# Split keys and queries kept in DRAM in the order of the stationary rows, each part twice, and loaded with one transfer over 128 partitions

## What is computed

```python
def _L0_xattn_ref(query, key, value, adj, mask, ...):
    Q, K, V = heads(query, Wq, bq), heads(key, Wk, bk), heads(value, Wv, bv)   # (B, 16, 512, 16)
    scores = einsum('bhqd,bhkd->bhqk', Q, K) / sqrt(16)
    scores = where(mask == 0, -inf, scores + adj)
    out = einsum('bhqk,bhkd->bhqd', softmax(scores), V)
    ...
x = x + _L0_attn_ref(_layernorm(x), ...)                  # Mamba-2
x = x + _L0_xattn_ref(_layernorm(x), ctx_1024, ctx_1024, adj, mask, ...)
x = x + _L0_ffn_ref(_layernorm(x), ...)
```

## Time and profile before

| | us |
|---|---|
| median of 3 runs | 1343.73 (1340.27 to 1345.88) |
| span of the profiled execution | 1348.2 |
| TensorE busy in it | 1190.5 (88%) |
| VectorE, ScalarE, GpSimd busy | 1001.0, 778.5, 635.0 |

### The profile page before, as it was taken

How to read it: one execution, slowest core, us unless ns; L and a number is a source line. 1 busy time by engine, 2 the same in 40 slices (tenths; PEclk the granted TensorE clock), 3 DMA queues, 4 the chain that set the end, 5 groups by cost and what they waited for, 6 DMA issues and landing times. The chain is left out here.

```text
span 1348.2 us, 29867 instructions
## 1 busy us (share of the span) xinstructions
PE 1190.5 (88%) x10284; PEld 833.2 (62%) x10284; DVE 1001.0 (74%) x2529; ACT 778.5 (58%) x1444; POOL 635.0 (47%) x554
## 2 busy tenths in 40 slices
PE   5688999899979999899989998999989998977387
PEld 2355567676757676666757665767767676755244
DVE  5767787788867887778767886888867886655386
ACT  2125577567655676557746766667545765566232
POOL 4561474346631683346532773168234663120365
PEclk9788899999988999889988999999988998899699
DMA  6043114300531033201430053104220142011511
GB/s 194 1 110 85 35 44 106 107 21 25 142 102 33 24 95 102 75 8 60 113 102 25 25 142 103 33 25 108 74 81 21 29 107 79 25 48 33 196 55 73
DMA packets 101524, 96.52 MB, mean 72 GB/s; under 512 B 17184, under 2 KB 76832, under 8 KB 100096
## 3 DMA queue, kind: packets, MB, share of 16 engines
q1 hardware_dynamic: 92912, 76.42, 19.0%
q0 software_dynamic: 6240, 17.57, 5.5%
q10 hardware_dynamic: 2224, 0.62, 0.2%
HBM read 71.49 MB, written 27.26 MB: 73 GB/s over the span
## 5 line engine op out<-in xcount | busy, mean ns | idle before, releaser
L891 ACT ACTIVATE T<-T,nmx 128x512 f32<-128x512 f32 x512 | 368.8, 724 | 249.2 <-DVE nmx L1257 245.8
L1257 DVE CUSTOM_DVE_ANT_0 T<-ps,am 128x512 f32<-128x512 f32 x512 | 346.6, 685 | 151.5 <-PE ps L680 149.6
L688 PE MATMUL pt<-ident,T 128*128 128x128 f32 x2048 | 336.4, 290 | 14.0 <-ACT PT L882 13.2
L688 PEld LDWEIGHTS pt<-ident,T 128*128 128x128 f32 x2048 | 240.2, 147 | 123.2 <-issue 93.4
L882 ACT COPY PT<-pt 128x512 f32<-128x512 f32 x352 | 201.8, 573 | 15.9 <-PE pt L688 15.2
L680 PE MATMUL ps<-k_st,q_st 64*128 64x512 f32 x512 | 135.8, 523 | 60.4 <-DMA q_st<-q_d 29.8
L1373 POOL TENSOR_TENSOR dmask<-triu,dA 128x1024 fp32r<-128x1024 f32 x64 | 132.1, 2129 | 49.7 <-DVE dA L1101 49.6
L705 PE MATMUL po<-PT,va 128*32 128x128 f32 x4096 | 140.1, 278 | 10.2 <-issue 6.2
L680 PEld LDWEIGHTS ps<-k_st,q_st 64*128 64x128 f32 x512 | 50.3, 192 | 136.4 <-issue 43.9
L1411 POOL TENSOR_TENSOR rr<-se,nhalf 128x1 f32<-128x1 f32 x32 | 22.2, 693 | 234.1 <-DVE se L1187 220.1
L705 PEld LDWEIGHTS po<-PT,va 128*32 128x32 f32 x4096 | 106.1, 110 | 33.2 <-issue 32.1
(11 more groups left out here) (212 smaller groups left out, 2030.1 us busy)
## 6 DMA issues: line engine op xcount, KB each, us to landing
k_st<-k_d SPq DMA_DIRECT2D x256, 64.0 KB, 2.2
q_st<-q_d SPq DMA_DIRECT2D x256, 64.0 KB, 2.4
am<-in_mask SPq DMA_DIRECT2D x8, 1024.0 KB, 5.4
k_d<-kp SPq DMA_DIRECT2D x32, 256.0 KB, 2.6
am<-in_adj POOLq DMA_DIRECT2D x8, 1024.0 KB, 10.6
q_d<-qp SPq DMA_DIRECT2D x128, 64.0 KB, 1.6
x_in<-in_x SPq DMA_DIRECT2D x8, 512.0 KB, 4.4
ctx_in<-in_ctxT SPq DMA_DIRECT2D x8, 512.0 KB, 4.5
```

Of the source, the lines that this page charges most:

```text
L688: ins = pe.transpose(pt[u % 2][:, kt * P:(kt + 1) * P], T[:, u % RING, kt * P:(kt + 1) * P], ident[:, :])
L891: act.activation(T[:, u % RING, :], T[:, u % RING, :], ACT.Exp, bias=nmx[:, u % RING:u % RING + 1], scale=-1.0).then_inc(sems["probs"], 1)
L1257: dve.tensor_tensor_reduce(T[:, u % RING, :], ps[(a * UNITS + u) % S_BANKS][:, :], ams[a % 2][:, qt, :], -1.0, 3e38, ALU.add, ALU.min, nmx ...
```

## The change

The DRAM tensors get the shape of the rows: `q_d[b, tile, pair, head of pair, copy, number, query]` and `k_d[b, pair, head of pair, copy, number, key]`. Each part is stored twice, to the two copies that hold it, with the loop over channel halves outside and over the four copies inside. A load is then one transfer over 128 partitions. A k store goes from 4 transfers of 256 KB to 8, a q store from 4 of 64 KB to 8; a key group is loaded with 1 transfer in place of 8, a query tile with 1 of 512 KB in place of 8 of 64 KB. The bytes loaded stay, the bytes stored double. Semaphore counts follow.

```diff
-        q_d = nc.dram_tensor("q_d", (B, C, 2, E, P), F32, kind="Internal").ap()
-        k_d = nc.dram_tensor("k_d", (B, 2, E, S), F32, kind="Internal").ap()
+        q_d = nc.dram_tensor("q_d", (B, C, HP, 2, 4, AD, P), F32, kind="Internal").ap()
+        k_d = nc.dram_tensor("k_d", (B, HP, 2, 4, AD, S), F32, kind="Internal").ap()
...
                 def k_in(b, g):
-                    for r, hl in enumerate((0, 1, 0, 1)):
-                        src = k_d[b, hl, g * HG * AD:(g + 1) * HG * AD, :].rearrange("(n h d) s -> h d n s", h=2, d=AD)
-                        for h in range(2):
-                            sp.dma_start(k_st[(4 * h + r) * AD:(4 * h + r + 1) * AD, HG // 2 * g:HG // 2 * (g + 1), :].bitcast(F32),
-                                         src[h]).then_inc(sems[f"k_in{g}"], 16)
+                    n = slice(HG // 2 * g, HG // 2 * (g + 1))
+                    sp.dma_start(k_st[:, n, :].bitcast(F32), k_d[b, n].rearrange("n h r d s -> (h r d) n s")).then_inc(sems[f"k_in{g}"], 16)
 
                 def q_in(b, c):
-                    for r, hl in enumerate((0, 0, 1, 1)):
-                        src = q_d[b, c, hl].rearrange("(n h d) s -> h d n s", h=2, d=AD)
-                        for h in range(2):
-                            sp.dma_start(q_st[(4 * h + r) * AD:(4 * h + r + 1) * AD, c % 2, :, :].bitcast(F32), src[h]).then_inc(sems[f"q_in{c % 2}"], 16)
+                    sp.dma_start(q_st[:, c % 2, :, :].bitcast(F32), q_d[b, c].rearrange("n h r d s -> (h r d) n s")).then_inc(sems[f"q_in{c % 2}"], 16)
...
                     if k == "rload":
-                        sp.wait_ge(sems["k_out"], at("k_out", b, 16 * 4))
+                        sp.wait_ge(sems["k_out"], at("k_out", b, 16 * 8))
...
-                        for hl in range(2):
-                            for kt in range(KE):
-                                sp.dma_start(k_d[b, hl, kt * P:(kt + 1) * P, :], kp[:, hl, kt, :].bitcast(F32)).then_inc(sems["k_out"], 16)
+                        for kt in range(KE):
+                            for r, hl in enumerate((0, 1, 0, 1)):
+                                sp.dma_start(k_d[b, HP // KE * kt:HP // KE * (kt + 1), :, r].rearrange("n h d s -> (n h) d s"), kp[:, hl, kt, :].bitcast(F32)).then_inc(sems["k_out"], 16)
...
-                        for hl in range(2):
-                            for kt in range(KE):
-                                sp.dma_start(q_d[b, c, hl, kt * P:(kt + 1) * P, :], qp[:, hl, kt, :].bitcast(F32)).then_inc(sems["q_out"], 16)
+                        for kt in range(KE):
+                            for r, hl in enumerate((0, 0, 1, 1)):
+                                sp.dma_start(q_d[b, c, HP // KE * kt:HP // KE * (kt + 1), :, r].rearrange("n h d s -> (n h) d s"), qp[:, hl, kt, :].bitcast(F32)).then_inc(sems["q_out"], 16)
...
-                        dve.wait_ge(sems["q_out"], at("q_out", b, 16 * 4 * c))
+                        dve.wait_ge(sems["q_out"], at("q_out", b, 16 * 8 * c))
```

More of the change, by code:

```diff
@@ L308, in build @@
             stats2=C, mean_var2=C, var_eps2=C, rstd2=C, query_normed=C, x1_bias=C, k_high=2, k_low=2, q_biased=C, q_high=C, q_low=C,
-            v_half=2, mask_bias=C, score_bias=16, k_out=16 * 4, q_out=16 * 4 * C,
-            k_in0=16 * 8, k_in1=16 * 8, k_in2=16 * 8, k_in3=16 * 8, q_in0=16 * 16, q_in1=16 * 16, score=UNITS, row_max=UNITS, probs=UNITS, turned=UNITS, evac_act=C * (AH - len(EVAC_DVE)), evac_dve=C * len(EVAC_DVE),
+            v_half=2, mask_bias=C, score_bias=16, k_out=16 * 8, q_out=16 * 8 * C,
+            k_in0=16, k_in1=16, k_in2=16, k_in3=16, q_in0=16 * 2, q_in1=16 * 2, score=UNITS, row_max=UNITS, probs=UNITS, turned=UNITS, evac_act=C * (AH - len(EVAC_DVE)), evac_dve=C * len(EVAC_DVE),
             pv=GROUPS, sums_out=C, sums_turned=C, recip=C, heads_normed=C,
@@ L477, in m @@
                         c = stg[1]
-                        sp.wait_ge(sems["q_out"], at("q_out", b, 16 * 4 * (c + 1)))
+                        sp.wait_ge(sems["q_out"], at("q_out", b, 16 * 8 * (c + 1)))
                         sp.wait_ge(sems["score"], at("score", b, AH * (c - 1)))
@@ L674, in score @@
                     if h == 0:
-                        pe.wait_ge(sems[f"q_in{qt % 2}"], at(f"q_in{qt % 2}", a, 16 * 8 * (qt // 2 + 1)))
+                        pe.wait_ge(sems[f"q_in{qt % 2}"], at(f"q_in{qt % 2}", a, 16 * (qt // 2 + 1)))
                     if qt == 0 and h % HG == 0:
-                        pe.wait_ge(sems[f"k_in{h // HG}"], at(f"k_in{h // HG}", a, 16 * 8))
+                        pe.wait_ge(sems[f"k_in{h // HG}"], at(f"k_in{h // HG}", a, 16))
                     pe.wait_ge(sems["row_max"], at("row_max", a, u + 1 - S_BANKS))
```

## The result

| | us |
|---|---|
| before, measured beside it | 1344.81 (1340.27 to 1350.16) |
| after | 1409.99 (1405.36 to 1416.56) |
| ratio | 1.050, 95% interval 1.045 to 1.054 |
| span of the profiled execution | 1403.6 (before 1348.2) |

The change makes the kernel slower by 5%. The sign of the forecast (1352 us) was right; the size was not, and the time lies above its range. The sign is not to the forecast's credit: it hung on a difference of 8 us, and slower had a chance of 0.41. Lines of the changed kernel: scores 674, key stores 453, query stores 464, key loads 419, query loads 422, `x2_d` 478 (`x_d` in the rows, which leave numbers out of names).

The account below looks back on a forecast made before the run. TensorE, busy 88% of the span, was taken to bound the kernel, its stalls and low clock costing time. 1348.2 - 81 + 64.5 + 24.5 = 1356 us, scaled 1352; own range 1340 to 1364, with rivals A and C 1305 to 1378.

Parts of the forecast that it names:

- key waits: Score of the fifth head, batches 1 to 7: the wait for key group 1 goes, 28.7 us gained.
- low clock around them: TensorE after the fifth-head key wait: 7.55 us at half speed goes, 3.8 us times 7, 26 us gained.
- waits of tile 1: Score of query tile 1, batch 0 apart: waits for the query load go, 5.4 us gained.
- low clock in tile 1: TensorE in tile 1: it lasts 36.35 us in place of up to 41.2, 19 us gained over six batches.
- waits of tile 3: Score of tile 3: new query-load waits, 9.5 us in six batches and about 7.5 in batch 0, 64.5 us lost.
- low clock behind them: TensorE after each new tile-3 wait: low clock of 3.5 us, 24.5 us lost in all.
- waits of tile 0 and tile 2: Scores of tiles 0 and 2: no added wait; tile 0's store-to-score chain was taken as unchanged.
- the time of the key stores on 8 engines: Key stores ahead of the tile-3 query load: 11.0 us of packets, ending 12.6 us after the old issue time.
- rival A: Tile-3 query load slips through ahead of `adj`: waits of 4 us in six batches, 1318 us, scaled 1313; chance 0.22.
- The chains held to be neutral: Query store followed by load (tile 0; tiles 2 and 3 at the end): 8.9 to 9.5 us, no change, 0.5 either way.
- rival C: Query load as one transfer takes over 5 us: tile 2 waits 0.4 us plus low clock, 22 us more, 1373; chance 0.13.
- B: Stores go over 16 shares, the tile-3 query load lands in time, gains stand alone: 1267 us, scaled 1263; chance 0.13.

Follow-up runs that it names:

- experiment 3: The changed kernel with the `adj` load cut to 32 columns of one row block (16 KB of 1 MB): 1364.72 us, one run.
- experiment 1: The changed kernel with the number index put outside the copies in `k_d` and `q_d`, so a store has 128 rows outermost: 1280.24 us, ratio 0.954.
- experiment 2: The changed kernel with SyncE's due time of the key store moved behind the tile-3 query load, stores still over 8 engines: 1336.47 us, ratio 0.995.
- experiment 4: The row order of experiment 1, with both copies of a part written by one store that reads its source twice: 1253.02 us, ratio 0.935.
- experiment 7: Experiment 1 with only the query rows back in the changed kernel's order, so query stores go over 8 engines: 1328.0 us, ratio 0.988.

## Why the prediction failed, point by point

The forecast and what the two profiles show, as sums over all batches from score to score:

| term | forecast | measured |
|---|---|---|
| key waits | -28.7 | -28.7 |
| low clock around them | -26 | -16.6 |
| waits of tile 1 | -5.4 | -3.3 |
| low clock in tile 1 | -19 | -11.1 |
| batch 0 | -2 | in the other rows |
| waits of tile 3 | +64.5 | +90.8 |
| low clock behind them | +24.5 | +12.5 |
| waits of tile 0 and tile 2 | 0 | +6.3, +5.5 |
| sum | +8 | +55.4 |

In batches 1 to 7 the tile-1 waits went as forecast; batch 0, which was to gain 2 us, has 2.2 us more of them (4.3 in place of 2.1).

**Right.** The key wait is gone to the last tenth; the stores go over 8 engines (0.51); the `adj` load is in the way (experiment 3); and the tile-3 score waits in batches 0 to 6 (experiments 1 and 2 take away the spread and the place in the queue, and each time the wait goes).

**The term that failed: the time of the key stores on 8 engines, and by it the length of the tile-3 wait, 9.5 us for 13.3.** By the prediction's own clock, which starts at the old issue time of the key store (3.34 us after the q store, so 355.54 here), the q load was to land at 21.2 and landed at 25.0. Experiment 3 divides the difference. With `adj` out of the way the score still waits 7.6 us (mean of batches 1 to 6), where the prediction's sum for that case, rival A, gave 4: it had the stores' part 3.5 us too small. `adj` adds 5.7 us, and was forecast to add 5.5 (21.2 - 15.7). Three steps of the stores were too small. The four query stores added were priced at 0.475 us an issue, all eight at 3.67; they took 4.88, and the key store was issued 2.15 us later and not 0.85. The first packets of the keys followed 1.2 us after that (358.90) and not 0.75. (At 340.87 the row that the 0.75 was read from shows the first packets, 3 tenths; its full slices begin at 341.0.) And their 2.1 MB take an estimated 12.7 us at the 165 GB/s measured, where the prediction had 11.0: it gave each engine the pace of 381 GB/s over 16, 23.8, and 165 over 8 is 20.6. Why an engine is slower there stays open. The tile-3 waits are 26 of the 47 us that the forecast lacks. Of the rest, 17 us are low clock whose gain did not come, 12 the waits of tile 0 and tile 2, and 4 the other rows; against them the low clock behind tile 3 was priced 12 us too high.

**`adj` was priced right, by another course.** I let the stores be through at 12.6 and `adj` run from 12.8 for 6.5 us undisturbed. It came at 12.05 (367.59), met stores that were not through, and shared the engines with them: 10.8 us, to 22.8 instead of 19.3, and 2.2 us from there to the landing (forecast 1.9). But while it shared, the stores and most of the query load moved too, so that taking it out gains little more than was forecast. That the two prices agree to 0.2 us is in part luck.

**The chains held to be neutral.** Tile 0 was to take 8.9 to 9.5 us from the first store's issue to the score. In batch 2 it takes 403.78 to 414.26 = 10.48: 4.89 of issue (forecast 3.67), 1.59 until the load is issued (1.2 to 1.4), 4.00 of load (3.8 to 4.4). The issue lies 1.2 us above its price, the step to the load 0.2, and the load within. Tile 2 has the same chain: 0.35 to 0.81 us in batches 1 to 6, and 2.6 more in the last batch. That is the wait that rival C named, but from the stores' issue and not from a slow load (4.3 us to landing), and without the low clock that I gave it. Together 11.8 us; experiments 4 and 7 show that they hang on the query store, for the most part on its issue.

**The clock.** Behind the tile-3 stalls I took 3.5 us each; 0.9 to 1.5 us were paid behind those of batches 1 to 6 (5.9 behind that of batch 0). The clock does fall to 0.50 during the stall, but the work after it runs at that level for only some 3.4 us (mean 0.77 over 380.6 to 388). Around the fifth head, the gain of 22.5 us behind it (forecast 26) is partly given back ahead of it: with the longer tile-0 wait there is low clock in the first four heads, 5.9 us in all. And tile 1 keeps 38.0 us in batches 1 to 6 instead of 36.35: a 3.4 us stretch of low clock (from 452.23 in batch 2) remains, with no idle time over 0.15 us from the start of the tile to it. So that low clock was not the price of the tile-1 wait alone, as I read it from rows 4 and 5. Of the 11.1 us gained, 6.5 are in the last batch. (In the kernel before, tile 1 lasts 16.1 us more than 36.35 over batches 1 to 6 together; the 19 us of the forecast can't be added up from those.) Experiment 4 has the low clock no more in most batches (36.43, clock 1.00); what brings it stays open.

**The rivals.** B, 16 shares at 1263 us, is what experiment 1 shows for the other index order: 1280.24. The mechanism and most of its price were right. A (the load slips through ahead of `adj`) did not occur: `adj` came before the query load was issued at all (367.59 and 369.55).

## What to carry to other kernels

A layout in DRAM that makes loads cheap must be looked at from the store's side too: here the outermost index of the stores decided over how many engines they went, and the order of two indices was worth 9% of the time. When a store gets slower, look for what stands behind it in the same queue and what the other queue starts meanwhile, and price all of the store: the issues ahead of it, the time to its first packets, and the pace of its bytes. Where the price of a part is doubtful, take that part out in a run, as experiment 3 did with `adj`. If one source goes to two places, one transfer that reads it twice may replace two.

## What was not expected of the hardware

- The issue of a store grows with its spread over fewer engines: 0.61 us for 64 KB on 8 engines and 0.455 on 16 (4.88 and 3.64 for eight); 1.14 us for 256 KB on 8, 0.66 on 16 beside the same number of bytes (9.10 and 5.26 for eight). The bytes of the keys take longer than their issues (2.1 MB at 165 GB/s: 12.7 us), so there the queue can hold the issues back, which no run here shows; those of the queries don't (0.52 MB at that rate: 3.2 us), and why these are slower stays open.
- A store whose source is read twice (experiment 4) keeps the full rate, 351 GB/s against 361 for two stores, and costs half of the issues.
- A load through GpSimd's queue, 6.5 us with 93.3% of the engines, takes 10.8 us beside a SyncE queue with work, at 59.5%.
